# One unit of scores and one weighted unit between the groups of maxima, in the second halves of an attention kernel's head groups

## The chip, the cores and the metric

The kernel runs on one core of one Trainium2 chip. The metric is the time of one execution on the device in microseconds (us); less is better. Times come from three runs of the kernel, and one further execution was recorded by the hardware profiler.

## What is computed

The reference is one hybrid layer over 4 sequences of 1024 tokens of width 512: attention, a feed-forward layer with experts, a state-space mixer, and the experts again. The change touches attention alone:

```python
kqv = (x @ Wqkv + bqkv).reshape(b, s, 3, 16, 32)
q, k, v = kqv[:, :, 0], kqv[:, :, 1], kqv[:, :, 2]
scores = jnp.einsum('bsnh,btnh->bnst', k, q) / math.sqrt(32)
scores = jnp.triu(scores) + -10000.0 * jnp.tril(ones, k=-1)
attn = jax.nn.softmax(scores, axis=2)
out = jnp.einsum('bnkq,bknh->bqnh', attn, v)
return out.reshape(b, s, 512) @ Wo + bo
```

There are 16 heads of 32 columns, and the scores are causal: a key is used only by queries at or behind it.

## The kernel before

Each engine has its own program, written out by hand; the engines meet through semaphores alone. A loop runs over the 4 batches. In a batch, attention goes over 4 groups of 4 heads (`g`), each in two halves of 2 heads (`hf`); such a half is a pair, so there are 8 pairs in a batch and 32 in all. The pair's number over the whole run is `p`.

For each pair the work is of these kinds:

- **Groups of maxima** (`group_scores_a`, matmuls on L872 and L877). TensorE computes scores with the queries on the partitions, preceded by mask matmuls, into PSUM banks 0 and 1. VectorE reduces each query's row to its maximum (L1675). The sixteen tiles of a pair (2 heads by 8 tiles of queries) are packed into nine groups, `MAX_GROUPS`, numbered 0 to 8, each filling up to 1024 columns. All nine use the same two banks, so a group waits on `a_max` until VectorE is done with all groups before it. They are computed one pair ahead: while pair p is worked off, the maxima of pair p + 1 are formed. This is not done in a batch's last pair (`ahead` is false there).
- **The turn of the maxima** (`turn_maxima`, L902). The maxima are transposed, copied by ScalarE (L1287) and sent by DMA into an extra row of QS, so that the next scores come out with the maximum already subtracted.
- **Units of scores** (`scores_b`, L915 masks and L919). The second set of scores, keys on the partitions, in 12 units; `ORDER` lists them as (half of the queries, tile of the keys). Their widths are 512, 128, 256, 384, 512, 128, 256, 384 and four times 512 columns, for two heads each. Even units go to banks 2 and 3, odd ones to banks 4 and 5. A unit u waits on `ex` until ScalarE has exponentiated unit u - 2.
- **Exponentials** (`exponentials`, L1313). ScalarE reads a unit's two banks and writes PR, which has four buffers.
- **Weighted units** (`weigh`, L934 with the values V and L936 with ones, for the sums). They accumulate in bank 6. Units 0 to 3 make up the first half of the queries, units 4 to 11 the second. Each matmul appears as two records in the trace. A unit waits for its own exponential, and a unit with s == 0 (units 0 and 4), which starts a new accumulation in bank 6, also waits for ScalarE's copies of what stood there before:

```python
ex.wait(pe, p, u + 1)
if s == 0:
    o_copied.wait(pe, p, c)
```

`Signal.wait(n, k)` waits for count `n * per + k`, and one increment at the start is added on both sides. `o_copied` has two increments a pair, so unit 0 of pair p waits until both halves of all pairs before it are copied, and unit 4 until pair p's own first half is.

ScalarE copies bank 6 out in `take`: `den` (L1322; den is another name of the tile xh) and OT (L1323). Its order around a change of pairs is the exponentials of units 0 and 1 of the new pair, `take` of the old pair's second half, in some sessions a conversion of outputs (`output_hi`, L1329), then the exponentials of units 2 and 3. `take` of the first half stands in session 1, behind the exponentials of units 4 and 5.

A pair is worked off in five sessions k. `FILLING` gives a session its groups of maxima, (0, 1), (2, 3), (4, 5), (6, 7), (8,), and `WEIGHED` its weighted units, (0, 1), (2, 3), (4, 5), (6, 7) and (8, 9, 10, 11). TensorE's order in a session is: a group of maxima; units of scores 2k + 2 and 2k + 3; in first halves (`hf == 0`) of the first three groups a chunk of the next group's projection (`project`, L756 to L758); the second group of maxima; two weighted units. Units 0 and 1 are scored at the end of the pair before (L1004, `scores_b(p + 1, pair + 1, (0, 1))`).

VectorE follows the same sessions: the maxima of each group, and reciprocals of the sums (`invert`, L1687) between them. SP issues the DMAs that place the heads' rows in QS and KS (`stack`); TensorE waits for them ahead of groups 0 and 4.

Of the kernel before, what the change touches and what calls it, by code (L numbers as in the profile page):

```python
# [36 lines left out]
SESSIONS = 5  # L37
WEIGHED = [(0, 1), (2, 3), (4, 5), (6, 7), (8, 9, 10, 11)]
# [4 lines left out]
FILLING = [(0, 1), (2, 3), (4, 5), (6, 7), (8,)]  # L43
# [10 lines left out]
def home(pair, hh):  # L54
    return (2 * pair + hh) % HOMES
# [6 lines left out]
def mrow_count(pair):  # L62

    return sum(mrow_parts(q) for q in range(pair % 2, pair + 1, 2))
# [10 lines left out]
def score_bank(u):  # L75
    return 2 + u % 2 * 2


def span(u):

    c, s = ORDER[u]
    t0 = max(c * HB, s * P)
    return c, s, t0, (c + 1) * HB - t0
# [83 lines left out]
def hybrid_layer(nc, x, Wqkv, bqkv, Wo, bo, W_in, conv_w, conv_b, z_bias, Dskip, W_out,  # L167
                 Wr, br, Wd, bd, Wu, bu, out):
    with ExitStack() as ctx:
# [553 lines left out]
        def _(pe):  # L723
# [30 lines left out]
            def three(dst, hi_l, lo_l, hi_r, lo_r, first, last):  # L754

                pe.matmul(dst, hi_l, hi_r, start=first, stop=False)  # L756
                pe.matmul(dst, hi_l, lo_r, start=False, stop=False)  # L757
                return pe.matmul(dst, lo_l, hi_r, start=False, stop=last)  # L758
# [66 lines left out]
            with pe.Fori(0, NB) as b:  # L825
# [20 lines left out]
                def project(g, ch, first=False):  # L846

                    w, c = ch // 2, ch % 2
                    if ch == 0:
                        qkw_lo.wait(pe, b * 4 + g, 1)  # L850
                    elif not first:
                        pj_lo.wait(pe, b * 4 + g, ch)
                    cols = slice(c * HB, (c + 1) * HB)
                    for k in range(KT):
                        i = three(ps[:, 4 + ch if first else 7, :], win[:, 0, w, 0, k, :], win[:, 0, w, 1, k, :],
                                  uh[:, k, cols], ul[:, k, cols], k == 0, k == KT - 1)
                    i.then_inc(pj.sem, 1)
# [3 lines left out]
                def scores_a(pair, tiles):  # L861

                    begun = set()

                    def first_of(at):
                        new = at // HB not in begun
                        begun.add(at // HB)
                        return new

                    for hh, t, off in tiles:  # L870
                        at = off + t * P
                        pe.matmul(flat[:, at:at + P], identb[:, :], mask_ts[:, :], start=first_of(at), stop=False, skip_group_check=True)  # L872
                    for hh, t, off in tiles:
                        n = (t + 1) * P
                        for c in range(0, n, HB):
                            m = min(HB, n - c)
                            i = pe.matmul(flat[:, off + c:off + c + m], QS[0:STACK, home(pair, hh), t * P:(t + 1) * P],  # L877
                                          KS[0:STACK, home(pair, hh), c:c + m], start=first_of(off + c), stop=True, skip_group_check=True)
                        i.then_inc(a_pe.sem, 1)
# [11 lines left out]
                def group_scores_a(p, pair, j):  # L891

                    tiles = MAX_GROUPS[j]
                    if j in (0, 4):
                        pe.wait_ge(s_stack[pair % 2][j // 4], (b * 4 + pair // 2) * 96 + 96)
                    if j:
                        a_max.wait(pe, p, sum(len(x) for x in MAX_GROUPS[:j]))
                    scores_a(pair, tiles)

                def turn_maxima(p):  # L900
                    a_max.wait(pe, p, 16)
                    pe.transpose(ps[0:2 * TT, 0, 0:P], mneg[:, :, :].rearrange("p h t -> p (h t)"), ident[:, :]).then_inc(m_pe.sem, 1)  # L902

                def scores_b(p, pair, units):

                    for u in units:
                        c, s, t0, n = span(u)
                        if u == 0:
                            pe.wait_ge(s_mrow[pair % 2], b * (MROWS * 16) + mrow_count(pair) * 16)
                            if pair == 1:  # L910
                                pe.wait_ge(s_kone, b * 2 + 2)
                        ex.wait(pe, p, max(u - 1, 0))
                        if s * P >= c * HB:
                            for hh in range(2):
                                pe.matmul(ps[:, score_bank(u) + hh, 0:P], identb[:, :], mask_st[:, :], start=True, stop=False, skip_group_check=True)  # L915
                    for u in units:
                        c, s, t0, n = span(u)
                        for hh in range(2):
                            i = pe.matmul(ps[:, score_bank(u) + hh, 0:n], KS[:, home(pair, hh), s * P:(s + 1) * P],  # L919
                                          QS[:, home(pair, hh), t0:t0 + n], start=s * P < c * HB, stop=True, skip_group_check=True)  # L920
                        i.then_inc(st_pe.sem, 1)

                def weigh(p, g, hf, u):

                    c, s, t0, n = span(u)
                    at = t0 - c * HB
# [3 lines that stand above are left out]
                    last = u == UNITS - 1 or ORDER[u + 1][0] != c  # L930
                    for hh in range(2):
                        h = g * P + (2 * hf + hh) * HS
                        o, r = hf * 64 + hh * HS, (1 - hf) * 64 + hh * HS
                        pe.matmul(ps[o:o + HS, 6, at:at + n], V[:, s, h:h + HS],  # L934
                                  PR[:, u % 4, hh, 0:n], start=(s == 0), stop=last)
                        i = pe.matmul(ps[r:r + HS, 6, at:at + n], ones[:, 0:HS],  # L936
                                      PR[:, u % 4, hh, 0:n], start=(s == 0), stop=last)
                    i.then_inc(pv.sem, 1)
# [42 lines left out]
                for g in range(GROUPS):  # L981
                    for hf in range(2):
                        p = b * 8 + g * 2 + hf
                        pair = g * 2 + hf
                        ahead = (g, hf) != (GROUPS - 1, 1)
                        for k in range(SESSIONS):
                            if ahead:
                                group_scores_a(p + 1, pair + 1, FILLING[k][0])
                            if k == 0:
                                scores_b(p, pair, (2,))  # L990
                                scores_b(p, pair, (3,))
                            else:
                                scores_b(p, pair, (2 * k + 2, 2 * k + 3))
                            if hf == 0 and g < GROUPS - 1 and k < 4:
                                project(g + 1, k)
                            if ahead:
                                for j in FILLING[k][1:]:
                                    group_scores_a(p + 1, pair + 1, j)
                            if k == SESSIONS - 1 and ahead:
                                turn_maxima(p + 1)  # L1000
                            for u in WEIGHED[k]:
                                weigh(p, g, hf, u)
                        if ahead:
                            scores_b(p + 1, pair + 1, (0, 1))  # L1004
# [56 lines left out]
                for t in range(2 * KT):  # L1061
# [7 lines left out]
                    for c in range(2):  # L1069
                        for k in range(KT):  # L1070
                            i = three(ps[:, XZ_BANK[t] + c, :], win[:, t % 2, 0, 0, k, :], win[:, t % 2, 0, 1, k, :],
                                      uh[:, k, c * HB:(c + 1) * HB], ul[:, k, c * HB:(c + 1) * HB], k == 0, k == KT - 1)
# [1002 lines left out]
```

## Time and profile before

| | |
|---|---|
| Three runs | 3100.57, 3096.14, 3099.93 us; median 3099.93 us |
| The profiled execution | 3103.92 us |
| Its span | 3102.2 us |
| Mean granted clock of TensorE over the span | 0.979 of full speed |
| The changed pairs | 12 of 32 pairs, each some 24.3 us from one turn of maxima to the next |

The profile is one execution of the program. The busy shares are averages over stages with different limits; idle time is given with what released the engine. A timeline row has the start and the duration in us, the engine, the line of the kernel, and the operation with output and inputs; `xN` joins N of them, and the brackets give the idle time before it and what ended it. A matmul's recorded duration includes its tail, in which the next one is already running, so the time that a block holds TensorE is read from start to start.

### The profile page before, as it was taken

To read this page: it belongs to the slowest core of one execution; us is meant where nothing else is said; L and a number is where in the kernel's file an instruction comes from. 1 tells how busy PE (TensorE), PEld (TensorE's weight loads), DVE (VectorE), ACT (ScalarE), POOL (GpSimd) and SP (SyncE) were. 2 spreads that over 40 slices of the span, in tenths; PEclk is the share of its full clock that TensorE was granted. 3 is DMA by queue.
4 is the path that set the end of the run, shared out by engine and by line. 5 is a ranking of instruction groups with operands and counts; after the bars stand their busy time and mean duration, and the time that the engine had idled before them with its cause. 6 is when DMAs were issued, how large, how long until landed. Compare 5 with 4: busy or idle time off the path is not lost.

```text
span 3102.2 us, 58883 instructions
## 1 busy us (share of the span) xinstructions
PE 2868.8 (92%) x20916; PEld 2084.0 (67%) x20916; DVE 1941.5 (63%) x2910; ACT 1204.2 (39%) x1913; POOL 756.0 (24%) x1045
## 2 busy tenths in 40 slices
PE   3899999999999999999989989999998999999998
PEld 3655577777665557777765547777776555777775
DVE  2555565777745563777665547477776555657777
ACT  2244334444135433444323452444421444344442
POOL 3301113333111111333311111233322011123331
PEclk7899999999999999999999999999999999999999
DMA  9323111111232202111133220211123230111112
GB/s 349 87 61 67 32 48 43 52 47 50 78 84 61 46 18 62 46 48 46 40 97 76 49 46 18 68 52 47 39 70 89 49 79 15 52 52 48 45 45 79
DMA packets 163781, 192.05 MB, mean 62 GB/s; under 512 B 43962, under 2 KB 103994, under 8 KB 161786
## 3 DMA queue, kind: packets, MB, share of 16 engines
q1 hardware_dynamic: 156126, 175.57, 20.8%
q10 hardware_dynamic: 7456, 13.90, 1.4%
q8 instruction: 116, 1.90, 0.3%
q14 instruction: 83, 0.68, 0.1%
HBM read 106.99 MB, written 23.36 MB: 42 GB/s over the span
## 4 chain that ended last, share of the span: by engine, by line
PE 69%; DVE 12%; issue 8%; DMA 3%; SPq 3%; ACT 2%; POOL 1%; ACTq 1%; DVEq 0%; POOLq 0%
PE ps L756 15%; PE ps L757 14%; PE ps L758 14%; PE ps L877 4%; DVE mneg L1675 4%; PE ps L1125 4%; PE ps L934 3%; PE ps L919 2%; PE ps L1111 2%; PE ps L872 2%; PE ps L1134 2%; PE ps L1171 2%; DMA win_raw<-in_t 1%; ACT PR L1313 1%; PE ps L766 1%
## 5 line engine op out<-in xcount | busy, mean ns | idle before, releaser
L756 PE MATMUL ps<-uh,win 128*128 128x512 f32 x1536 | 625.1, 407 | 17.2 <-POOL win L1920 16.5
L757 PE MATMUL ps<-ul,win 128*128 128x512 f32 x1536 | 602.7, 392 | 0.0
L758 PE MATMUL ps<-uh,win 128*128 128x512 f32 x1536 | 601.5, 392 | 0.0
L1675 DVE TENSOR_REDUCE mneg<-ps 128x1 f32<-128x896 f32 (+7 forms) x512 | 367.5, 753 | 361.7 <-PE ps L877 360.1
L1313 ACT ACTIVATE PR<-ps 128x1024 f32<-128x1024 f32 (+3 forms) x384 | 293.2, 807 | 317.4 <-PE ps L919 290.6
L756 PEld LDWEIGHTS ps<-uh,win 128*128 128x128 f32 x1536 | 289.6, 189 | 92.2 <-POOL win L1920 19.4
L758 PEld LDWEIGHTS ps<-uh,win 128*128 128x128 f32 x1536 | 289.4, 188 | 64.8
L2016 POOL TENSOR_SCALAR_AFFINE_SELECT LM<-LM 128x512 f32<-128x512 f32 x256 | 208.9, 827 | 492.4 <-ACT LM L1428 492.4
L757 PEld LDWEIGHTS ps<-ul,win 128*128 128x128 f32 x1536 | 290.3, 189 | 53.6
L1789 DVE TENSOR_TENSOR LM<-ps,LM 128x512 f32<-128x512 f32 x256 | 170.3, 686 | 242.8 <-PE ps L1125 198.5
L934 PE MATMUL ps<-PR,V 128*32 128x512 f32 (+3 forms) x1536 | 282.4, 492 | 5.0 <-ACT OT L1323 2.7
L936 PE MATMUL ps<-PR,ones 128*32 128x512 f32 (+3 forms) x1536 | 282.3, 492 | 0.0
L1777 DVE SCALAR_TENSOR_TENSOR Ct<-ps,cpt,Ct 128x1023 f32<-128x1023 f32 (+2 forms) x192 | 245.6, 1279 | 14.4 <-ACT Ct L1418 9.9
L1777 DVE SCALAR_TENSOR_TENSOR Bt<-ps,cpt,Bt 128x1023 f32<-128x1023 f32 (+2 forms) x192 | 243.7, 1269 | 1.9 <-ACT Bt L1418 1.6
L1920 POOL TENSOR_TENSOR win<-win_raw,win 128x512 fp32r<-128x512 f32 (+1 forms) x49 | 82.1, 1679 | 616.7 <-ACT win L1250 332.4
L1224 ACT CAST uh<-ps 128x512 fp32r<-128x512 f32 x128 | 73.6, 587 | 373.3 <-PE ps L766 373.3
L877 PE MATMUL ps<-KS,QS 96*128 96x512 f32 (+3 forms) x768 | 213.4, 377 | 0.0
L1428 ACT ACTIVATE LM<-ps 128x512 f32<-128x512 f32 x256 | 147.5, 601 | 124.2 <-PE ps L1111 124.1
L919 PE MATMUL ps<-QS,KS 97*128 97x512 f32 (+3 forms) x768 | 189.8, 364 | 1.4 <-ACT PR L1313 1.4
L934 PEld LDWEIGHTS ps<-PR,V 128*32 128x32 f32 x1536 | 79.0, 109 | 141.9 <-issue 92.9
L1687 DVE RECIPROCAL xh<-xh 128x128 f32<-128x128 f32 x128 | 116.1, 931 | 79.9 <-ACT OT L1323 79.9
L1418 ACT ACTIVATE Ct<-ps,cpt 128x1024 f32<-128x1024 f32 x64 | 77.2, 1207 | 207.7 <-PE ps L758 207.7
(228 smaller groups left out, 5150.8 us busy)
## 6 DMA issues: line engine op xcount, KB each, us to landing
raw<-in_t SPq DMA_DIRECT2D x128, 256.0 KB, 2.8
QS<-EV SPq DMA_DIRECT2D x192, 128.0 KB, 2.5
KS<-EV SPq DMA_DIRECT2D x168, 128.0 KB, 2.6
in_t<-tiles ACTq DMA_DIRECT2D x10, 1024.0 KB, 9.6
XN<-in_L_attn_a_x_dram SPq DMA_DIRECT2D x40, 256.0 KB, 5.2
win_raw<-in_L_attn_a_Wqkv_dram SPq DMA_DIRECT2D x34, 256.0 KB, 3.3
win_raw<-in_t SPq DMA_DIRECT2D x32, 256.0 KB, 2.8
edec<-ed_t SPq DMA_DIRECT2D x512, 16.0 KB, 1.6
```

Source lines behind the costliest of these rows:

```text
L756: pe.matmul(dst, hi_l, hi_r, start=first, stop=False)
L757: pe.matmul(dst, hi_l, lo_r, start=False, stop=False)
L758: return pe.matmul(dst, lo_l, hi_r, start=False, stop=last)
L877: i = pe.matmul(flat[:, off + c:off + c + m], QS[0:STACK, home(pair, hh), t * P:(t + 1) * P], KS[0:STACK, home(pair, hh), c:c + m], start= ...
L919: i = pe.matmul(ps[:, score_bank(u) + hh, 0:n], KS[:, home(pair, hh), s * P:(s + 1) * P], QS[:, home(pair, hh), t0:t0 + n], start=s * P < ...
L934: pe.matmul(ps[o:o + HS, 6, at:at + n], V[:, s, h:h + HS], PR[:, u % 4, hh, 0:n], start=(s == 0), stop=last)
L936: i = pe.matmul(ps[r:r + HS, 6, at:at + n], ones[:, 0:HS], PR[:, u % 4, hh, 0:n], start=(s == 0), stop=last)
L1313: act.activation(PR[:, u % 4, :, 0:n], ps[:, score_bank(u):score_bank(u) + 2, 0:n], ACT.Exp, scale=SCALE).then_inc(ex.sem, 1)
L1675: dve.tensor_reduce(mneg[:, hh, t:t + 1], flat[:, off:off + (t + 1) * P], AX.X, ALU.max, negate=True).then_inc(a_max.sem, 1)
L1777: dve.scalar_tensor_tensor(dst[:, par, k:L], wide(2 * w)[:, 0:L - k], cpt[:, par, w, at:at + 1], dst[:, par, k:L], ALU.mult, ALU.add).then ...
L1789: dve.tensor_tensor(LM[:, q, :], ps[:, 5 + q % 2, :], LM[:, q, :], ALU.mult).then_inc(m_dve.sem, 1)
L2016: pool.affine_select(out=v, in_=v, compare_op=ALU.is_ge, fill=0.0, base=0, pattern=[[0, 4], [1, P]], channel_multiplier=-1).then_inc(sel_p ...
```

## The change

In the second half of a group, where the next pair's maxima are formed, the first four sessions have another order on TensorE: a group of maxima, one unit of scores, one weighted unit, the second group of maxima, one unit of scores, one weighted unit. The fifth session, the first halves, the last pair of a batch and the programs of the other engines are unchanged.

```diff
                         for k in range(SESSIONS):
                             if ahead:
                                 group_scores_a(p + 1, pair + 1, FILLING[k][0])
+                            if hf == 1 and ahead and k < SESSIONS - 1:
+                                for i in range(2):
+                                    scores_b(p, pair, (2 * k + 2 + i,))
+                                    weigh(p, g, hf, WEIGHED[k][i])
+                                    if i == 0:
+                                        group_scores_a(p + 1, pair + 1, FILLING[k][1])
+                                continue
                             if k == 0:
                                 scores_b(p, pair, (2,))
                                 scores_b(p, pair, (3,))
```

## Rows read from the trace of the kernel before

**Rows 1.** The page: busy us, share of the span and instructions of each engine.

```profile
PE 2868.8 (92%) x20916; PEld 2084.0 (67%) x20916; DVE 1941.5 (63%) x2910; ACT 1204.2 (39%) x1913; POOL 756.0 (24%) x1045
```

**Rows 2.** Waits of TensorE: waiting line, releaser, total us, times, longest us.

```profile
PE ps L872 <- DVE mneg L1675: 47.0, 166, 0.8
...
PE ps L934 <- ACT OT L1323: 2.7, 8, 0.4
```

**Rows 3.** Timeline of TensorE, second half of group 1, first batch.

```profile
231.08 0.59 PE L934 MATMUL ps<-PR,V 128*32 128x512 f32 x1
...
232.05 0.40 PE L915 MATMUL ps<-mask_st,identb 128*128 128x128 bf16 x4
...
232.97 0.23 PE L872 MATMUL ps<-mask_ts,identb 128*128 128x128 bf16 x1
...
234.08 0.28 PE L915 MATMUL ps<-mask_st,identb 128*128 128x128 bf16 x2 [0.35 <-ACT PR L1313]
...
234.50 0.29 PE L915 MATMUL ps<-mask_st,identb 128*128 128x128 bf16 x2
...
235.05 0.28 PE L872 MATMUL ps<-mask_ts,identb 128*128 128x128 bf16 x2
...
235.78 0.62 PE L934 MATMUL ps<-PR,V 128*32 128x512 f32 x1
...
237.24 0.28 PE L872 MATMUL ps<-mask_ts,identb 128*128 128x128 bf16 x2 [0.17 <-DVE mneg L1675]
...
237.89 0.29 PE L915 MATMUL ps<-mask_st,identb 128*128 128x128 bf16 x2
...
239.43 0.29 PE L872 MATMUL ps<-mask_ts,identb 128*128 128x128 bf16 x2 [0.56 <-DVE mneg L1675]
...
241.67 0.28 PE L872 MATMUL ps<-mask_ts,identb 128*128 128x128 bf16 x2 [0.17 <-DVE mneg L1675]
...
243.87 0.29 PE L872 MATMUL ps<-mask_ts,identb 128*128 128x128 bf16 x2 [0.51 <-DVE mneg L1675]
```

**Rows 4.** Timeline of VectorE, the same pair.

```profile
233.76 1.23 DVE L1675 TENSOR_REDUCE mneg<-ps 128x1 f32<-128x1024 f32 x1 [5.55 <-PE ps L877]
235.89 1.29 DVE L1675 TENSOR_REDUCE mneg<-ps 128x1 f32<-128x896 f32 x2 [0.90 <-PE ps L877]
238.08 1.29 DVE L1675 TENSOR_REDUCE mneg<-ps 128x1 f32<-128x768 f32 x2 [0.90 <-PE ps L877]
```

**Rows 5.** Timeline of ScalarE, the same pair.

```profile
233.00 1.30 ACT L1313 ACTIVATE PR<-ps 128x1024 f32<-128x1024 f32 x2 [2.38 <-PE ps L919]
234.32 0.58 ACT L1322 COPY xh<-ps 64x512 f32<-64x512 f32 x1
234.92 0.58 ACT L1323 COPY OT<-ps 64x512 f32<-64x512 f32 x1
...
241.57 0.58 ACT L1322 COPY xh<-ps 64x512 f32<-64x512 f32 x1 [1.54 <-PE ps L936]
```

**Rows 6.** Timeline of TensorE, last pair of the first batch.

```profile
342.95 0.62 PE L934 MATMUL ps<-PR,V 128*32 128x512 f32 x1 [0.35 <-ACT OT L1323]
```

**Rows 7.** Timeline of ScalarE, last pair of the first batch.

```profile
342.32 0.58 ACT L1323 COPY OT<-ps 64x512 f32<-64x512 f32 x1
```

**Rows 8.** Timeline of TensorE, second half of group 2, fourth batch.

```profile
2549.76 0.40 PE L915 MATMUL ps<-mask_st,identb 128*128 128x128 bf16 x4
...
2551.35 0.23 PE L872 MATMUL ps<-mask_ts,identb 128*128 128x128 bf16 x1 [0.50 <-DMA KS<-EV]
...
2553.42 0.28 PE L872 MATMUL ps<-mask_ts,identb 128*128 128x128 bf16 x2 [0.36 <-DVE mneg L1675]
```

**Rows 9.** Stretches: from:to, length, busy us by engine, granted clock (PEclk), DMA share, GB/s.

```profile
core 0: us, PE busy (x) PEld busy (x) DVE busy (x) ACT busy (x) POOL busy (x), PEclk, DMA share, GB/s
232.00:252.00 20.00, 17.62 (x148) 10.62 (x144) 12.67 (x18) 11.15 (x17) 3.64 (x2) 1.00 0.46 106
339.00:345.00 6.00, 4.29 (x43) 2.38 (x36) 0.00 (x0) 4.16 (x7) 1.26 (x1) 1.00 0.00 0
88.00:92.00 4.00, 3.73 (x9) 2.97 (x10) 2.33 (x9) 0.27 (x1) 1.20 (x2) 0.50 0.47 180
```

## The prediction

> **What bounds the kernel now.** I read the page's busy shares first: TensorE is busy for 2868.8 us of 3102.2 us [rows 1], so at first sight its own work is the bound. That average does not hold for the stage that is changed, so the waits of TensorE come next: the mask matmuls that open a group of maxima (L872) waited 47.0 us in all, 166 times, for the maxima of VectorE [rows 2]. Then I read the three engines' timelines over one pair of heads of the changed kind, the second half of group 1 in the first batch, 232 to 252 us [rows 3 to 5]. Below, A0 to A8 are the groups of maxima, B2 to B11 the units of scores, W0 to W11 the weighted units, and k0 to k4 the five sessions.
>
> In that pair the groups start at 235.05, 237.24, 239.43, 241.67 and 243.87 us, 2.19 to 2.24 us apart, whatever TensorE does between them [rows 3]. VectorE explains it: A1 starts at 235.05, its maxima start at 235.89 and take 1.29 us, to 237.18, and A2 starts at 237.24; A2's maxima run from 238.08 to 239.37, and A3 starts at 239.43 [rows 3, 4]. Each group writes the two PSUM banks that the maxima before it read, so this is one serial chain: about 0.84 us of scores, 1.29 us of maxima, 0.06 us until TensorE goes on. Of the 2.19 us TensorE has 0.65 us for the group itself (237.24 to 237.89 [rows 3]) and some 1.5 us for whatever else is queued. Today that is two scores or two weighted units, and it idles after both: 0.56 us before A3, 0.51 us before A5, 0.17 us before A2 and A4 [rows 3].
>
> **What the change does, part by part.** No instruction is added or removed. In 12 of the 32 pairs (second halves of groups 0, 1 and 2, four batches), in k0 to k3, the order A, B, B, A, W, W becomes A, B, W, A, B, W. DMAs and the queues of SP and POOL keep their content; ScalarE and VectorE keep their order. The moved steps are W(2k), now ahead of the session's second group, and B(2k+3), now behind it. The waits come along: W0 needs the exponential of unit 0 and also, since it opens an accumulation in bank 6, that ScalarE has copied out the previous pair's second half (o_copied, L929). W4 needs the same of this pair's first half.
>
> **Session 0, the term that decides.** A0 stands at 232.97 us. B2 starts at 234.08, after 0.35 us of waiting for unit 0's exponential, and takes 0.42 us, to 234.50 [rows 3]. Next in the new queue is W0. ScalarE has its queue in this order: exponentials of units 0 and 1 from 233.00, then the two copies of bank 6 at 234.32 and 234.92, the second ending at 235.50 [rows 5]. Before, W0 came at 235.78 and the wait was hidden. How soon W0 follows the copy is seen in the last pair of the batch, which has no maxima: the copy starts at 342.32 [rows 7] and W0 at 342.95, after 0.35 us of recorded waiting for it [rows 6], so 0.63 us after the copy's start; the kernel has 2.7 us of this wait, 8 times [rows 2]. In the changed pair W0 then starts at 234.92 + 0.63 = 235.55 us. A weighted unit of 512 columns holds the queue for 0.97 us (W11 of the pair before starts at 231.08, the next block at 232.05 [rows 3]). So A1, queued behind W0, starts at 236.52 instead of 235.05: 1.47 us later. Behind the blocked W0 stand A1, hence VectorE's next maxima, and B3, hence unit 3's exponential.
>
> Ten of the twelve pairs look like this. In two, both in group 2 of a late batch, A0 itself waits for the DMA of KS and A1 is already late: the block before starts at 2549.76, A0 at 2551.35, A1 at 2553.42 [rows 8]. The copy follows the block's start by 234.92 - 232.05 = 2.87 us [rows 3, 5], so W0 would come at 2549.76 + 2.87 + 0.63 = 2553.26 and A1 at 2554.23, 0.81 us later than now.
>
> **Does the chain give it back?** I take nothing back. From A1 on each step is bound by VectorE, with no slack in which a late start could be made up: the maxima follow each group at the same distance, and the last group releases the transposition of the maxima and with it the end of the pair. The next pair starts from there.
>
> **Sessions 1 to 3**, cost taken as 0. The longest half is k2's first: A4 0.65, B6 at 0.42 (the width of B2), W4 0.97, and 0.08 for going from scores to weighted units (A1 to W0 took 0.73, A2 to B4 0.65 [rows 3]): 2.12 us, against the 2.20 us from A4 to A5 that the maxima need anyway (241.67 to 243.87 [rows 3]). Cover 0.08 us. W4 also waits for the copies of the first half, which start once W3 is done (241.57 now, 0.10 us ahead of A4 [rows 3, 5]). The two copies and the release take 0.60 + 0.63 = 1.23 us by the starts used above, so W4 can start about 1.13 us after A4 if W3 ends as now. TensorE arrives 0.65 + 0.42 + 0.08 = 1.15 us after A4. These are the thinnest covers of the plan. If they fail, A5 is late by perhaps 0.1 to 0.3 us a pair, 1.2 to 3.6 us in all. From below, a gain in these sessions is excluded as long as the maxima set the step: TensorE's idle time is only moved, from behind the scores to both halves. B3, B5, B7 and B9 come later than now, B3 by 2.7 us (from 234.50 to 236.52 + 0.65). Most of their exponentials are asked for a whole session later, 4.4 us. The shortest is unit 9's, which B11 wants right behind A8: B9 ends about 1.2 us after A7, its exponential takes at most 1.30 us (two together, [rows 5]), and B11 comes 2.19 + 0.65 = 2.84 us after A7. That holds, so I put it at 0.
>
> **Sum.** 10 x 1.47 + 2 x 0.81 = 16.3 us. The profiled execution took 3103.92 us (span 3102.2), 3.99 us or 0.13% above the median of the three runs, 3099.93, so the sum is set against the execution as 3120.2 and against the median as 3116.2 us, 0.53% slower. About 0.2% (6 us) is what a measurement of this kernel can tell from no change.
>
> **The rivals.**
> - *The copy is no obstacle* (chance 0.05). If W0 waited for the exponential alone, A1 would come at 234.08 + 0.42 + 0.08 + 0.97 = 235.55, 0.50 us late, and in the two late pairs not at all: 5.0 us, 3104.9 us. For it: in the changed pairs today nothing is seen of the wait on the copy. Against it: rows 6 and 7 show just that wait, with the same code and the same order on ScalarE.
> - *Faster: the even split fills the idle time* (0.05). Two weighted units in a row would then be what delays every second group. If all of the recorded idle time went, 0.56 before A3, 0.51 before A5, as much for A7, and 0.17 before each of the five others, it would be 2.4 us a pair, 29 us in twelve; less the 16.3 us, some 13 us faster, 3087 us. It decides if a group can start sooner than 0.06 us after the maxima have ended. Rows 3 and 4 are against it: A2 and A3 both follow the end of the maxima by 0.06 us, one behind weighted units, one behind scores.
> - *A second stall in k2* (0.08): the thin covers above fail, 1.2 to 3.6 us more, up to 3119.8 us.
> - *The clock falls* (0.03). The granted clock is 1.00 in the changed pair and also in the last pair's stretch, where TensorE is busy for only 4.29 of 6 us; at 88 to 92 us it was 0.50, which is the 1.2 GHz level [rows 9]. If the new stall brought it down once a pair, the late half of session 0 after it (0.65 + 0.42 + 0.97 = 2.04 us of work) would take twice as long: 24.5 us more, 3140.7 us. The Trainium skill, "TensorE: Matmul & The Clock Gate", section "A second HAM failure mode: psum-queue depth-cycling", says that short idle spells between groups of matmuls can make the clock swing between its levels. By that rule 3140.7, by the row of the last pair 3116.2; the trace does not show the rule at work here.
>
> That the change does nothing is hardly possible: its condition is met in 48 sessions, and the order of the queue is what TensorE executes.
>
> **How the numbers follow.** Forecast 0.79, rivals 0.05, 0.05, 0.08, 0.03. The likeliest is 3116.2. The forecast's own bounds: 0.81 us in all twelve pairs gives 9.7 us and, with the median at 3100, 3109.7; 1.5 us in all, plus 3.6 of a second stall and 2 us of scatter gives 3123.5. I take 3109 to 3123.5, which holds the forecast and the k2 rival. Faster 0.05, same 0.05, slower 0.90.
>
> **What would show it.** In the changed kernel's timeline W0 in the second halves starts 0.63 us after the OT copy, with a recorded wait on ScalarE's OT, and A1 4.47 us after the block B0, B1 began (now 3.00). From A1 on the groups stay 2.19 to 2.24 us apart, and the distance between the transpositions of maxima grows by about 1.5 us in these pairs only. TensorE's waits gain a row for L934 on OT of some 8 to 12 us. Wrong would be: groups closer than 2.19 us, W0 before the copy ends, a clock below 1.00 in these pairs, or first halves that change too.

## The result and the profile after

The changed kernel takes 3115.67 us (median of 5 runs, 3106.81 to 3124.17) against 3099.93 us: ratio 1.0053 with a 95% interval of 1.0032 to 1.0075. That is 15.7 us slower; 3116.2 us had been forecast. The interval allows 10 to 23 us, so the agreement of the medians within 0.5 us is luck; the account by pairs below is the better test. The profiled execution took 3124.17 us (span 3122.4 us).

The busy shares of the changed kernel's page are within a point those of before [rows 1], in a longer span:

```profile
PE 2882.8 (92%) x20916; PEld 2081.1 (67%) x20916; DVE 1940.6 (62%) x2910; ACT 1209.8 (39%) x1913; POOL 756.5 (24%) x1045
```

The waits of TensorE (releaser, total us, times, longest us) show what changed. Lines behind the edit have moved by 7, so L1682 is the maxima's L1675 and L1330 the OT copy's L1323.

```profile
PE ps L872 <- DVE mneg L1682: 42.5, 138, 0.8
...
PE ps L934 <- ACT OT L1330: 13.2, 20, 0.9
```

Beside rows 2 the wait on the OT copy has grown from 2.7 us in 8 times to 13.2 us in 20: twelve new waits, one for each changed pair. Eleven are of 0.89 us; one, behind a late A0, is of 0.78. The wait on the maxima has shrunk by 28 times and only 4.5 us.

Here is TensorE in the second half of group 1 of the first batch, the pair of rows 3:

```profile
231.69 0.40 PE L915 MATMUL ps<-mask_st,identb 128*128 128x128 bf16 x4
...
232.63 0.23 PE L872 MATMUL ps<-mask_ts,identb 128*128 128x128 bf16 x1
...
233.73 0.28 PE L915 MATMUL ps<-mask_st,identb 128*128 128x128 bf16 x2 [0.36 <-ACT PR L1320]
...
235.20 0.62 PE L934 MATMUL ps<-PR,V 128*32 128x512 f32 x1 [0.89 <-ACT OT L1330]
...
236.20 0.29 PE L872 MATMUL ps<-mask_ts,identb 128*128 128x128 bf16 x2
...
238.39 0.28 PE L872 MATMUL ps<-mask_ts,identb 128*128 128x128 bf16 x2 [0.49 <-DVE mneg L1682]
...
240.58 0.28 PE L872 MATMUL ps<-mask_ts,identb 128*128 128x128 bf16 x2 [0.34 <-DVE mneg L1682]
...
242.82 0.28 PE L872 MATMUL ps<-mask_ts,identb 128*128 128x128 bf16 x2 [0.24 <-DVE mneg L1682]
...
245.01 0.28 PE L872 MATMUL ps<-mask_ts,identb 128*128 128x128 bf16 x2
```

and ScalarE beside it:

```profile
233.98 0.58 ACT L1329 COPY xh<-ps 64x512 f32<-64x512 f32 x1
234.57 0.58 ACT L1330 COPY OT<-ps 64x512 f32<-64x512 f32 x1
```

Count from the start of the block B0, B1 (231.69). Weighted unit 0 starts at 3.51 us, 0.63 us after the start of the OT copy. Group A1 starts at 4.51 us, where the kernel before had 3.00 [rows 3]. From there on A2, A3, A4 and A5 follow at 2.19, 2.19, 2.24 and 2.19 us, no closer than before.

The clearest measure is the distance from one turn of the maxima (L902) to the next. It is 24.30 us for a changed pair before and 25.79 us after, for ten pairs; the two pairs with a late A0 go from 24.87 and 24.95 to 25.80.

| us, one execution each | before | after |
|---|---|---|
| the 12 changed pairs, turn to turn | 292.80 | 309.50 |
| the other pairs (16 distances) | 497.91 | 500.64 |
| between batches (3 distances) | 1667.60 | 1670.51 |
| start to the first turn | 137.53 | 135.66 |
| last turn to the end of the span | 506.34 | 506.14 |

Of the 20.2 us between the two executions, 16.7 lie in the changed pairs. The other pairs make up the next 2.7 us, all but 0.1 of it in two pairs in group 3 in which TensorE's clock fell; the rest is the sum of the last three rows, and nothing shows that it belongs to the change. The falls in group 3 are not shown to be an effect of the change: executions of kernels with the old order in all second halves have them too (two in that with the copies first, one in that with one copy more, both below). Stretches of the changed kernel around one of them (columns as in rows 9):

```profile
316.00:324.00 8.00, 6.86 (x59) 4.17 (x51) 4.64 (x6) 3.75 (x6) 1.27 (x1) 1.00 0.30 76
324.00:329.00 5.00, 4.44 (x29) 1.90 (x28) 2.83 (x5) 1.82 (x3) 0.00 (x0) 0.66 0.00 0
329.00:337.00 8.00, 6.98 (x62) 3.94 (x61) 6.82 (x10) 4.29 (x7) 2.38 (x2) 1.00 0.00 0
```

A granted clock of 0.66 over 5 us is 3.41 us at 1.2 GHz. That pair took 26.21 us instead of 24.89. It waited 0.79 and 0.56 us for the maxima just before the fall, as the same pair of the kernel before did without a fall.

### The profile page after: what moved, and what is told of

Same layout as the page of the kernel before. It is cut to its first block, busy times and chain, and to the rows that moved or that the text cites. A ratio compares the mean times of both kernels' runs of the same rounds, so it can differ in the third digit from the quotient of the medians.

```text
span 3122.4 us, 58883 instructions
## 1 busy us (share of the span) xinstructions
PE 2882.8 (92%) x20916; PEld 2081.1 (67%) x20916; DVE 1940.6 (62%) x2910; ACT 1209.8 (39%) x1913; POOL 756.5 (24%) x1045
## 4 chain that ended last, share of the span: by engine, by line
PE 70%; DVE 12%; issue 8%; SPq 3%; DMA 3%; ACT 3%; POOL 1%; ACTq 1%; DVEq 0%; POOLq 0%
PE ps L756 15%; PE ps L757 14%; PE ps L758 14%; PE ps L877 4%; PE ps L934 4%; PE ps L1132 4%; DVE mneg L1682 4%; PE ps L1118 2%; PE ps L919 2%; PE ps L872 2%; PE ps L1141 2%; PE ps L1178 2%; DMA win_raw<-in_t 1%; PE ps L766 1%; ACT PR L1320 1%
## 5 line engine op out<-in xcount | busy, mean ns | idle before, releaser
L756 PE MATMUL ps<-uh,win 128*128 128x512 f32 x1536 | 625.9, 407 | 16.5 <-POOL win L1927 15.7
L1682 DVE TENSOR_REDUCE mneg<-ps 128x1 f32<-128x896 f32 (+7 forms) x512 | 367.5, 753 | 380.7 <-PE ps L877 379.3
L934 PE MATMUL ps<-PR,V 128*32 128x512 f32 (+3 forms) x1536 | 293.3, 496 | 15.6 <-ACT OT L1330 13.2
L936 PE MATMUL ps<-PR,ones 128*32 128x512 f32 (+3 forms) x1536 | 293.3, 496 | 0.0
L919 PE MATMUL ps<-QS,KS 97*128 97x512 f32 (+3 forms) x768 | 197.4, 366 | 1.4 <-ACT PR L1320 1.4
```

The lines of the kernel that those rows point to most:

```text
L934: pe.matmul(ps[o:o + HS, 6, at:at + n], V[:, s, h:h + HS], PR[:, u % 4, hh, 0:n], start=(s == 0), stop=last)
L936: i = pe.matmul(ps[r:r + HS, 6, at:at + n], ones[:, 0:HS], PR[:, u % 4, hh, 0:n], start=(s == 0), stop=last)
L1682: dve.tensor_reduce(mneg[:, hh, t:t + 1], flat[:, off:off + (t + 1) * P], AX.X, ALU.max, negate=True).then_inc(a_max.sem, 1)
```

## The experiments

Three explanations stand against each other. In the **copy theory** weighted unit 0 waits for ScalarE's copy out of bank 6, and the second group of maxima is queued behind it. In the **exponential theory** it waits for unit 0's exponential alone. In the **switch theory** every change between kinds of matmuls costs a little, in all four sessions.

**The new order in session 0 alone.**

```diff
-                            if hf == 1 and ahead and k < SESSIONS - 1:
+                            if hf == 1 and ahead and k == 0:
```

> The new order in session 0 of the changed pairs alone; sessions 1 to 3 as before. Copy theory (weighted unit 0 is held back by ScalarE's copy out of bank 6 and the second group of maxima is queued behind it): the whole loss is here, 25.79 us from one turn of the maxima to the next in a changed pair where the kernel before has 24.30 (0.85 to 0.93 in the two late pairs), 16.7 us in all, about 3116 us. Switch theory (each change between kinds of matmuls costs some, in all four sessions alike): a quarter of it, 24.67 us a pair, about 3104 us. Exponential theory (unit 0 is held back by its exponential alone): 24.80 us a pair, 3105 us.

3118.08 us, ratio 1.0057 (1.0034 to 1.008). Nine of the changed pairs take 25.79 to 25.81 us; the three others, in which the clock fell, take 26.84, 27.21 and 27.21. The whole loss is in session 0.

**The new order in sessions 1 to 3 alone.**

```diff
-                            if hf == 1 and ahead and k < SESSIONS - 1:
+                            if hf == 1 and ahead and 0 < k < SESSIONS - 1:
```

> The new order in sessions 1 to 3 alone; session 0 as before. Copy theory: nothing is lost or won, 24.30 us a changed pair, within 2 us of the kernel before apart from stretches at the lower clock; the weighted unit 4 still comes just in time. Switch theory: three quarters of the loss, 25.4 us a pair, about 3112 us.

3101.57 us, ratio 1.0006 (0.9991 to 1.002), and 24.30 us a pair (24.29 to 24.31 in nine). In the other three, all in group 2, A0 waited for the DMA of KS, as in the two late pairs of the kernel before, and they take 24.83 to 25.01 us. These sessions neither gain nor lose, though all their moves are in place. With the run before, this ends the switch theory.

**Unit 3 moved, weighted unit 0 not.**

```diff
                                 for i in range(2):
                                     scores_b(p, pair, (2 * k + 2 + i,))
-                                    weigh(p, g, hf, WEIGHED[k][i])
+                                    if k > 0:
+                                        weigh(p, g, hf, WEIGHED[k][i])
                                     if i == 0:
                                         group_scores_a(p + 1, pair + 1, FILLING[k][1])
+                                if k == 0:
+                                    for u in WEIGHED[k]:
+                                        weigh(p, g, hf, u)
                                 continue
```

> The changed kernel, but in session 0 both weighted units stand at the end: group, unit 2, group, unit 3, weighted 0, weighted 1. It keeps the move of unit 3 behind the second group and takes back the move of weighted unit 0. Copy theory: no loss, 24.30 us a pair. If the late unit 3 and its exponential were a part of the loss, the pair would be above 24.30 us; switch theory has about 25.5.

3106.13 us, ratio 1.0016 (1.0005 to 1.0028). Most changed pairs take 24.60 us, 0.30 above the expectation. TensorE's timeline, second half of group 0:

```profile
172.17 0.40 PE L915 MATMUL ps<-mask_st,identb 128*128 128x128 bf16 x4
...
174.21 0.29 PE L915 MATMUL ps<-mask_st,identb 128*128 128x128 bf16 x2 [0.36 <-ACT PR L1324]
...
175.17 0.28 PE L872 MATMUL ps<-mask_ts,identb 128*128 128x128 bf16 x2 [0.39 <-DVE mneg L1686]
175.82 0.29 PE L915 MATMUL ps<-mask_st,identb 128*128 128x128 bf16 x2
...
176.44 0.62 PE L934 MATMUL ps<-PR,V 128*32 128x512 f32 x1
...
177.66 0.28 PE L872 MATMUL ps<-mask_ts,identb 128*128 128x128 bf16 x2
```

A1 is back at 3.00 us. What I had not added up is the half behind it: the group 0.65, unit 3 0.62, weighted units 0 and 1 1.22 us make 2.49 us, and the maxima leave 2.19. A2 starts with no recorded wait, so here TensorE is the bound, by 0.30 us. A half can hold about 1.5 us of other work, and these three units are 1.84 us. One pair in group 2 took 27.77 us: its A0 waited for KS, its A1 then 0.90 us for the maxima, and the clock fell there, for 6.83 us, without any wait for a copy.

**ScalarE copies first, in the new order.** In the changed pairs `take` stands ahead of the exponentials of units 0 and 1:

```diff
+                        early = hf == 0 and g < GROUPS - 1
+                        if early:
+                            take(p, g, hf, 1)
                         if ahead:
                             for u in range(2):
                                 exponentials(p + 1, u)
-                        take(p, g, hf, 1)
+                        if not early:
+                            take(p, g, hf, 1)
```

> The changed kernel, with ScalarE copying bank 6 out ahead of the exponentials of units 0 and 1 in the changed pairs. The copies then end about 1.3 us after the block of units 0 and 1 begins instead of 3.45, and the exponential of unit 0 ends at 2.32 instead of 1.97. Copy theory: weighted unit 0 waits for no copy any more; unit 2 starts at 2.38, weighted unit 0 at 2.88, the second group at 3.85 (4.51 in the changed kernel, 3.00 before): 25.15 us a pair. If something else than the copy holds weighted unit 0, the pair stays at 25.8 us or gets longer by the 0.35 us of the later exponential, 26.1.

25.09 us a pair (3105.21 us, one run). TensorE's timeline:

```profile
170.45 0.40 PE L915 MATMUL ps<-mask_st,identb 128*128 128x128 bf16 x4
...
172.73 0.29 PE L915 MATMUL ps<-mask_st,identb 128*128 128x128 bf16 x2 [0.60 <-ACT PR L1320]
...
173.24 0.62 PE L934 MATMUL ps<-PR,V 128*32 128x512 f32 x1
...
174.24 0.28 PE L872 MATMUL ps<-mask_ts,identb 128*128 128x128 bf16 x2
```

Weighted unit 0 follows unit 2 without a wait, at 2.79 us, and A1 stands at 3.79 us instead of 4.51. So the copy was what held it, and about half of the loss (0.70 of 1.49 us a pair) goes with it.

**The same exchange in the kernel before**, as a control (the same diff).

> The kernel before with the same exchange on ScalarE, the control for the copy-first run. Its second group of maxima waits for units 2 and 3 alone, which start when the exponential of unit 0 is done: 2.38 instead of 2.03 us after the block of units 0 and 1 begins. Copy theory: 0.35 us lost a pair, 24.65 us, and so the new order costs only 0.5 us with the copies out of its way instead of 1.49. If the copies mattered to the old order too, the pair would get shorter than 24.30.

24.53 us a pair (3099.66 us, one run). TensorE's timeline:

```profile
172.87 0.40 PE L915 MATMUL ps<-mask_st,identb 128*128 128x128 bf16 x4
...
175.15 0.28 PE L915 MATMUL ps<-mask_st,identb 128*128 128x128 bf16 x2 [0.60 <-ACT PR L1313]
...
176.11 0.29 PE L872 MATMUL ps<-mask_ts,identb 128*128 128x128 bf16 x2
```

Unit 2 starts at 2.28 us, 0.25 later than before where 0.35 had been expected, and A1 at 3.24. The later exponential costs the old order 0.23 us a pair, so with the copies out of its way the new order costs 25.09 - 24.53 = 0.56 us: its remainder is weighted unit 0 itself (1.00 us, in the place of unit 3 with 0.54) in a half that already waits for an exponential.

**One copy more, in either order.**

```diff
                     act.copy(den[mine, c, :], ps[other, 6, :])
+                    if c == 1 and hf == 0 and g < GROUPS - 1:
+                        act.copy(spare[mine, :], ps[other, 6, :])
```

> The changed kernel with one more copy of the same size (0.58 us) in front of the OT copy, into a spare tile, in the changed pairs alone. Copy theory: every ns of it reaches the chain, 0.59 us more a pair, 26.4 us. Exponential and switch theory: nothing, 25.8 us.

> The kernel before with the same added copy. Weighted unit 0 comes 3.73 us after the block of units 0 and 1 begins and would now be let go at 4.09, and behind it there are 0.3 us until the maxima are done. Copy theory: 0.1 us a pair, 24.4 us; the added copy is nearly hidden here and fully seen in the new order.

In the old order weighted unit 0 now waits 0.18 us for the OT copy, and that is hidden: 24.30 to 24.32 us a pair in groups 0 and 1 (3101.9 us, one run). In group 2, where A0 came late, the pairs take 24.37 to 24.99. In the new order the pairs without a fall of the clock take 26.28 us, 0.49 more than in the changed kernel (3134.54 us, one run); 0.59 had been expected, but the added copy delays the OT copy by only 0.47 us. Only five of the twelve pairs are of this kind: in seven the clock falls, and they take 27.2 to 28.3 us. TensorE and its clock in one of these (second view as in rows 9):

```profile
175.65 0.48 PE L920 MATMUL ps<-QS,KS 97*128 97x256 f32 x2
177.51 0.62 PE L935 MATMUL ps<-PR,V 128*32 128x512 f32 x1 [1.38 <-ACT OT L1333]
...
177.96 0.84 PE L935 MATMUL ps<-PR,V 128*32 128x512 f32 x1
```

```profile
173.00:177.00 4.00, 2.78 (x23) 1.53 (x15) 1.23 (x1) 2.49 (x5) 0.00 (x0) 1.00 0.93 201
177.00:181.00 4.00, 3.49 (x17) 1.80 (x17) 0.84 (x1) 0.95 (x2) 0.00 (x0) 0.65 0.94 241
```

The second set of matmuls behind the 1.38 us of waiting already takes 0.84 us where it takes 0.59 at 2.4 GHz. In this pair the clock record falls 0.66 us behind the end of the stall.

**A version built on the reading**: more weighted units in the idle time of sessions 1 to 3. Session 0 is that of the run with unit 3 moved alone. In sessions 1 to 3 the weighted unit of each half is replaced by a list, and unit 8 is taken out of session 4:

```diff
+PULLED = {2: (2,), 3: (3,), 4: (4,), 5: (5, 6), 6: (7,), 7: (8,)}
...
-                                    weigh(p, g, hf, WEIGHED[k][i])
+                                    if k > 0:
+                                        for u in PULLED[2 * k + i]:
+                                            weigh(p, g, hf, u)
...
+                                if k == 0:
+                                    for u in WEIGHED[k]:
+                                        weigh(p, g, hf, u)
...
                             for u in WEIGHED[k]:
-                                weigh(p, g, hf, u)
+                                if not (hf == 1 and ahead and u == 8):
+                                    weigh(p, g, hf, u)
```

> A version built on the reading that VectorE's chain of maxima leaves TensorE idle in sessions 1 to 3: session 0 as in the run with both weighted units at its end, sessions 1 to 3 interleaved as in the changed kernel, but the weighted units 6, 7 and 8 each pulled forward by one gap (5 and 6 behind group 5, 7 behind group 6, 8 behind group 7), so that only 9, 10 and 11 are left after the turn of the maxima. If the gaps hold them (each needs up to 1.53 of 1.54 us by the rows), the groups keep their 2.19 to 2.24 us and the stretch from the turn of the maxima to the next block shrinks from 3.78 us to about 3.4, where the last exponential ends: 23.9 us a pair, 4.5 us in all faster than the kernel before, 3095.5 us. If a gap does not hold, a group starts 0.1 to 0.3 us late and the gain is gone.

3103.11 us, ratio 1.0014 (1.0002 to 1.0026): slower, a miss. The gaps do hold the units; the changed pairs of groups 0 and 1 take 24.62 to 24.65 us, near the 24.60 of the run with the same session 0. Those of group 2 take more: 25.19 and 25.33 us, where A0 waited for KS, and 26.73 and 26.76, where the clock fell as well. The shorter end shows in the pairs behind them: 33.11 instead of 33.46 and 24.42 instead of 24.91 us, but nothing behind group 0 (33.90). There the row of maxima goes out in two DMA issues on ScalarE (1.86 us, against 0.55 for the single one behind group 1), and the last exponential comes late anyway: the last weighted unit waits 1.52 us for it. The expectation had counted the gain in all three groups and had left out the 0.30 us that session 0 costs in this order.

**The same with session 0 as before** (`0 < k < SESSIONS - 1` in the condition).

> The pulled version with session 0 in the order of the kernel before. Chain theory: the 0.30 us that the run with both weighted units behind unit 3 and the pulled run lost in session 0 are gone (24.30 us a changed pair, 0.5 to 0.9 more in group 2 where KS is late), and the pairs that follow stay 0 (group 1), 0.35 (group 2) and 0.48 us (group 3) shorter as in the pulled run: 0.83 us a batch, 3.3 us in all, 3097 us. If the shorter end only moves the wait to the DMAs of KS, nothing is left, 3100 us.

3097.14 us, ratio 0.9996 (0.9986 to 1.0007). The pairs take 24.35 to 24.38 us in groups 0 and 1, 0.05 to 0.08 more than before, and those behind groups 1 and 2 keep their 0.36 and 0.48 us; in the traces that is some 2.8 us in all between the turns, too little for the measurement to tell. The end of a pair ahead of group 2 shows what limits it:

```profile
999.50 0.28 PE L903 MATMUL ps<-ident,mneg 128*16 128x128 f32 x1 [0.39 <-DVE mneg L1685]
...
1001.91 0.62 PE L935 MATMUL ps<-PR,V 128*32 128x512 f32 x1 [0.28 <-ACT PR L1323]
...
1002.90 0.29 PE L916 MATMUL ps<-mask_st,identb 128*128 128x128 bf16 x2
```

With one weighted unit less, the last one waits 0.28 us for its exponential, and the turn of the maxima to the next block takes 3.40 us, as worked out, where the kernel before has 3.78.

**The projection ahead of units 2 and 3**, in first halves, session 0:

```diff
+                            first = k == 0 and hf == 0 and g < GROUPS - 1
+                            if first:
+                                project(g + 1, k)
                             if k == 0:
                                 scores_b(p, pair, (2,))
                                 scores_b(p, pair, (3,))
...
-                            if hf == 0 and g < GROUPS - 1 and k < 4:
+                            if hf == 0 and g < GROUPS - 1 and k < 4 and not first:
```

> The kernel before, with one step moved in session 0 of the first halves of groups 0 to 2: the chunk of the projection stands ahead of units 2 and 3 instead of behind them. The trace has 0.35 to 0.36 us of recorded waiting (0.46 from start to start) of unit 2 for the exponential of unit 0 there, and the projection needs nothing of ScalarE. So the wait should be covered: 0.46 us less a pair in up to 12 pairs, 5.5 us in all, 3094.5 us. Against it: these first halves may be held by the maxima as the second ones are, then the 0.46 us come back as waiting before the third group and the time stays at 3100 us.

3098.59 us, ratio 0.9995 (0.9984 to 1.0006). In the trace the first halves of groups 1 and 2 are shorter by 0.46 to 0.54 us (33.86 for 34.34, 33.35 to 33.42 for 33.88 to 33.90, and 32.96 to 32.99 for 33.46), those of group 0 by 0.27: 5 us in all, in the place foreseen. By itself the measurement cannot tell it from nothing.

**Both together.**

> Both of the two versions sent with it. If they are independent: 8.8 us less than the kernel before, 3091 us; 3097 us if only the pulled units gain.

3090.45 us, ratio 0.9976 (0.9964 to 0.9988), 12 runs. This version beats both kernels: about 7.5 us less than before by the ratio, and 25 us less than the changed kernel by medians of different sets of runs. By the traces of the two versions alone 2.8 + 5.0 = 7.8 us were to be had; 8.8 had been expected.

## Why the prediction was right, point by point

- **The bound.** Maxima and groups form a serial chain of 2.19 to 2.24 us a step. The steps are the same in the changed kernel, and the run with sessions 1 to 3 alone shows that nothing is won there: 24.30 us a pair.
- **The term of session 0.** Forecast: weighted unit 0 0.63 us after the OT copy's start and A1 at 4.47 us. Measured: 0.63 us and 4.51 us; the difference is mainly weighted unit 0, which holds the queue for 1.00 us where 0.97 was taken from unit 11. The loss is 1.49 us a pair in ten (1.47 forecast) and 0.93 and 0.85 in the two late ones (0.81): 16.7 us against 16.3. How many pairs are late changes from one execution to the next: with session 0 in its old order A0 waits 0.3 us or more for KS in none to three of the four pairs of group 2. In the changed kernel the wait for the copy covers such a wait, and all its changed pairs take 25.78 to 25.80 us. The runs with session 0 alone, with the copies first and with one copy more show it in three ways: as a place, as a cause taken away, and as a cause made larger, which the new order hands on (0.49 us) and the old one hides.
- **The thin covers of session 2** held. In the pair shown, A5 starts 2.19 us after A4 with no recorded wait, so TensorE arrives just as the maxima end. Weighted unit 4 never waits for a copy, since the twenty waits on OT are eight in the last pairs of the batches, as before, and the twelve of unit 0.
- **Late units 3, 5, 7 and 9** cost nothing, as taken.
- **The rivals.** The exponential alone would have given 0.50 us a pair; with the copies out of the way the new order did cost 0.56. No idle time was won. The clock is the rival whose chance was too low. In the profiled execution of the changed kernel it fell at no new stall, though it fell twice in group 3. In the run with session 0 alone it fell in three of twelve pairs with the same stall, and with 0.49 us more in seven of twelve. So the chance of 0.03 was too low for a stall of this length, and that the profiled execution had no such fall is chance. A fall costs 0.9 to 1.4 us for one stretch of 3.41 us where the forecast had 2.04. Whether it adds to the scatter of the five runs (17 us) is not shown: five runs of the kernel before spread over 4 us, but the larger sets of its runs beside the experiments spread over 15 to 19 us.

## What to carry to other kernels

When a block is moved ahead in an in-order queue, list every semaphore it waits on, also those that never show in the profile because other work stood in front of them; a wait hidden in one place is the bound in another, and everything queued behind it pays. If two engines hand work to and fro, the step of that chain sets the time: spreading the rest evenly between its steps wins nothing (24.30 us a pair either way). Work taken from behind the chain into its gaps can win (0.36 and 0.48 us here, and nothing behind group 0), as long as each gap's sum stays below the step and nothing else holds the end. And work that waits for nobody, such as the projection here, belongs ahead of the work that waits.

## What the runs showed of the hardware that I had not expected

In this kernel one stall of about a microsecond between otherwise dense matmuls is enough, at times, for TensorE's clock to fall. In the changed pairs, with a recorded wait of 0.78 to 0.89 us for the copy, it stayed at 2.4 GHz in all twelve pairs of one execution; with 0.89 to 0.90 us it fell in three of twelve of another. With 1.38 us it fell in seven of nine; in that execution's other three pairs the wait, behind a late A0, was 1.23 to 1.33 us and the clock stayed. Each fall is to 1.2 GHz for 3.41 or 6.83 us, and begins between 0.14 us before and 0.97 us behind the end of the stall.

The stall need not be a wait for the copy: in the runs with weighted units 0 and 1 behind unit 3 there is no wait for a copy, and the clock fell in three pairs of group 2 where A0 waited for KS and A1 then 0.90 us for the maxima, while it stayed in two others like them. In the seven profiled executions with the old order in session 0 it never fell in the 84 changed pairs. In the first pair of group 3, which the change does not touch and which waits 0.79 and 0.56 us for maxima in a row, it fell 13 times in the 52 such pairs of all thirteen executions, though not in those of the kernel before.

The Trainium skill, "TensorE: Matmul & The Clock Gate", section "A second HAM failure mode: psum-queue depth-cycling", says that brief idle spells between groups of matmuls make the clock swing; the longer stall bears this out, and the last pair of the batch before the change [rows 9], with 4.29 of 6 us busy and no fall, shows that the spells alone do not decide it.
